# A two-layer graph attention kernel: masks built by ScalarE, a sum term in three bfloat16 parts, stacks loaded by fewer transfers, scores in column tiles

## The chip, the cores and the metric

The kernel runs on one core of a Trainium2 chip. The metric is the device time of one execution in microseconds (us); below it is the median of three runs. Lower is better.

## The reference, cut to what matters

Eight graphs (batches) of 1024 nodes with 128 features pass through two layers. Both use the same 0/1 adjacency matrix `adj`.

```python
# layer 0: 8 heads of 16 features
scores = einsum('bhqd,bhkd->bhqk', q, k) / sqrt(16)
w   = softmax(where(adj > 0, scores, -1e9))
x   = layernorm(x + (w @ v) @ Wo + bo)
# layer 1: one head
h   = x @ W.T
e   = leaky_relu(h @ a1 [:, :, None] + h @ a2 [:, None, :], 0.2)
x   = layernorm(x + softmax(where(adj > 0, e, -9e15)) @ h)
```

## The kernel before, in words

Everything stays on one core. A **unit** is the scores of one head and one block of 128 keys against all 1024 queries. There are 64 units in a batch, and unit `u` stands at **position** `u` of its batch. A unit has these steps:

- TensorE multiplies a 97-row stack of keys with a 97-row stack of queries: two matmuls of 512 columns (L415). The 97 rows are six blocks of 16 rows (q and k split into bfloat16 parts) and one row that subtracts a bound from the scores.
- ScalarE takes the exponential out of the PSUM slot into `weights` (L584).
- Non-neighbours are masked in one of two ways, chosen per unit by the string `MASKED_BY`. With "m" TensorE adds the mask to the scores with two more matmuls (L420). With "s" VectorE multiplies the weights by the mask afterwards (L755). "m" stands at 27 of the 64 positions.
- After each four units (a quad, four heads of one key block) TensorE adds their product with the values to the accumulator `acc` (L441). These are eight matmuls of 17 columns which stand in the four column tiles of the array, so that four run side by side.

Before a batch's units can run, its q and k are split into three bfloat16 parts each, written to a scratch in HBM (`send_parts`) and read back as the stacks `qst` and `kst` (`load_stack`), once for heads 0 to 3 and once for heads 4 to 7. The masks are made from the int32 adjacency rows (`raw`, two buffers), one for each key block (`make_mask`, L780, VectorE).

While the units of batch b run, the rest of batch b-1 (output projection, layer norm, layer 1) and of b-2 (the products `out0` to `out7` of layer 1, L474, and their final layer norm) is done between them, and q, k and v of batch b+1. What stands behind which position is written out by hand in one table for each engine (`PE_AT`, `ACT_AT`, `DVE_AT`, `POOL_AT`, `SP_AT`); an entry `("out0", -2)` at position 1 means: behind unit 1 of batch b, output product 0 of batch b-2. Each engine runs its list in order and waits on semaphores. Units and all jobs of TensorE that need PSUM share three slots in turn, so TensorE can be at most three uses ahead of the engines that empty them.

Each output product sums eight fp32 matmuls, and a ninth (L475) adds a constant row, the sum over all nodes times a tiny number, which keeps rows without neighbours defined: `pe.matmul(to, ones[:], hsum[:], ...)`, an fp32 product over 128 rows of which 127 are zero.

Of the kernel before, what the change touches and what calls it, by code (L numbers as in the profile page):

```python
# [35 lines left out]
}  # L36
PE_AT = {
# [4 lines left out]
}  # L42
ACT_AT = {
# [17 lines left out]
}  # L61

OFFSET_BITS = -70
EXPONENT = 40.0
FARTHEST = 60.0
# [7 lines left out]
def context_at(b, pos, batches):  # L73

    if pos % 4 != 3:
        return None
# [1592 lines left out]
```

## Time and profile before

| | |
|---|---|
| median of 3 runs | 927.75 us (924.52 to 927.9) |
| profiled execution, its own time | 921.75 us |
| its span, first to last instruction | 920.0 us |
| mean granted TensorE clock | 0.972 |
| busy: TensorE, VectorE, ScalarE, GpSimd | 844.0, 686.2, 635.3, 65.5 us |
| first exponential of the first unit | 37.75 us |
| first batch, second, third to seventh (each), eighth | 79.9, 93.0, 106.4, 98.6 us |
| from the last exponential of a unit to the end | 78.8 us |

The last three lines are start times of exponentials (L584), of position 0 in each batch. PE in a row is TensorE's matmuls, PEld its weight loads, DVE VectorE, ACT ScalarE, POOL GpSimd, SP the engine that issues the transfers. A matmul in fp32 shows as two records in the profile.

### The profile page before, as it was taken

What the parts mean: (1) busy time and instruction counts of PE and PEld (TensorE: products, weight loads), DVE (VectorE), ACT (ScalarE), POOL (GpSimd) and SP (SyncE); (2) the same over time, 40 slices, a digit from 0 to 9 for tenths busy, and PEclk for the clock granted to TensorE, in tenths of its full rate; (3) what the DMA queues carried; (4) which work ended last, traced back from release to release, by engine and by line L of the source; (5) the groups of instructions that cost most, each with busy time, mean ns of one, the idle gap of its engine ahead of it and who ended that gap; (6) DMA issues with size and microseconds to landing.
All of it is one profiled execution on the core that took longest, in us unless ns stands there. A gap on an engine that the chain in (4) does not pass through costs nothing.

```text
span 920.0 us, 14889 instructions
## 1 busy us (share of the span) xinstructions
PE 844.0 (92%) x5485; PEld 406.5 (44%) x5485; DVE 686.2 (75%) x1157; ACT 635.3 (69%) x702; POOL 65.5 (7%) x47
## 2 busy tenths in 40 slices
PE   5499999999999999999999999999999999998683
PEld 2132334327533474336543374334743366324573
DVE  5276797895878868896878868787687966796463
ACT  2378886995579846896579945898378965796050
POOL 3000010001010100101010010101010010101000
PEclk9599999999999999999999999999999999999877
DMA  4877258603556227544377136363275234401000
GB/s 158 158 135 154 38 163 161 111 7 109 110 120 105 81 92 94 138 58 126 82 149 100 39 102 118 115 94 90 83 136 110 44 105 96 54 2 35 1 24 26
DMA packets 50926, 85.56 MB, mean 93 GB/s; under 512 B 5969, under 2 KB 23122, under 8 KB 50834
## 3 DMA queue, kind: packets, MB, share of 16 engines
q1 hardware_dynamic: 50850, 84.57, 44.2%
q8 instruction: 45, 0.74, 0.4%
q14 instruction: 31, 0.25, 0.1%
HBM read 67.63 MB, written 16.91 MB: 92 GB/s over the span
## 4 chain that ended last, share of the span: by engine, by line
PE 69%; ACT 16%; issue 8%; DVE 5%; DMA 0%; POOL 0%; POOLq 0%; SPq 0%; ACTq 0%; DVEq 0%
PE acc L441 18%; PE slot L415 17%; PE slot L474 11%; ACT weights L584 11%; PE slot L420 8%; ACT atts L602 4%; PE slot L485 3%; PE slot L522 2%; PE slot L532 2%; DVE weights L755 1%; PE slot L475 1%; PE slot L458 1%; PE slot L512 1%; DVE atts L769 1%; PE slot L526 1%
## 5 line engine op out<-in xcount | busy, mean ns | idle before, releaser
L584 ACT ACTIVATE weights<-slot 128x1024 f32<-128x1024 f32 x512 | 496.1, 1048 | 169.4 <-PE slot L415 94.1
L755 DVE SCALAR_TENSOR_TENSOR weights<-mask,weights 128x1024 f32<-128x1024 bf16 x296 | 359.3, 1239 | 65.4 <-ACT weights L584 64.2
L415 PE MATMUL slot<-qst,kst 97*128 97x512 bf16 x1024 | 287.3, 383 | 26.9 <-issue 14.6
L441 PE MATMUL acc<-weights,vst 128*17 128x512 f32 x2048 | 244.6, 595 | 7.1 <-DVE weights L755 6.5
L415 PEld LDWEIGHTS slot<-qst,kst 97*128 97x128 bf16 x1024 | 84.7, 98 | 213.2 <-ACT weights L584 87.2
L420 PE MATMUL slot<-mask,same 128*128 128x512 bf16 x432 | 129.8, 381 | 0.0
L474 PEld LDWEIGHTS slot<-hst,atts 128*128 128x128 f32 x896 | 105.8, 191 | 19.4 <-issue 9.2
L474 PE MATMUL slot<-hst,atts 128*128 128x129 f32 x896 | 110.7, 276 | 3.0 <-ACT atts L602 3.0
L441 PEld LDWEIGHTS acc<-weights,vst 128*17 128x17 f32 x2048 | 47.9, 96 | 141.1 <-issue 127.5
L769 DVE SCALAR_TENSOR_TENSOR atts<-turn,hst,mask 128x1024 f32<-128x1024 f32 x64 | 83.5, 1310 | 6.8 <-ACT hst L652 6.8
L845 DVE RECIPROCAL rout<-slot 128x1 f32<-128x1 f32 x62 | 10.4, 167 | 91.0 <-PE slot L475 82.4
L602 ACT ACTIVATE atts<-atts,expbias 128x1024 f32<-128x1024 f32 x64 | 75.4, 1224 | 1.7 <-DVE atts L769 1.1
L420 PEld LDWEIGHTS slot<-mask,same 128*128 128x128 bf16 x432 | 42.4, 98 | 52.1 <-issue 1.1
L708 POOL TENSOR_TENSOR rstd<-vareps,exponent 128x4 f32<-128x4 f32 (+1 forms) x24 | 33.9, 1413 | 393.6 <-DVE vareps L825 393.6
L713 POOL TENSOR_TENSOR x_sb<-x_sb,bo_all 128x1024 f32<-128x1024 f32 x8 | 22.5, 2808 | 437.9 <-DMA x_sb<-in_x 437.9
L780 DVE TENSOR_SCALAR mask<-raw 128x1024 bf16<-128x1024 int32 x64 | 48.1, 753 | 6.4 <-DMA raw<-in_adjT 6.4
L618 ACT ACTIVATE atts<-slot 128x1024 bf16<-128x1024 f32 x16 | 16.4, 1023 | 23.6 <-PE slot L485 23.6
L830 DVE TENSOR_SCALAR x<-y,meanvar,rstd 128x128 f32<-128x128 f32 x64 | 17.1, 343 | 14.5 <-POOL rstd L708 14.5
L793 DVE TENSOR_TENSOR atts<-slot,atts 128x1024 f32<-128x1024 f32 x16 | 19.6, 1224 | 11.2 <-issue 11.0
L641 ACT ACTIVATE turn<-slot 128x1024 f32<-128x1024 f32 x8 | 8.2, 1023 | 26.0 <-PE slot L518 26.0
L846 DVE SCALAR_TENSOR_TENSOR x<-slot,rout,x 128x128 f32<-128x128 f32 x62 | 21.8, 351 | 2.2
L864 DVE TENSOR_REDUCE widest<-slot 64x1 f32<-64x1024 f32 x8 | 9.7, 1216 | 17.2 <-issue 10.0
(117 smaller groups left out, 580.3 us busy)
## 6 DMA issues: line engine op xcount, KB each, us to landing
raw<-in_adjT SPq DMA_DIRECT2D x64, 512.0 KB, 4.1
parts_scratch<-atts SPq DMA_DIRECT2D x48, 256.0 KB, 2.5
qst<-parts_scratch SPq DMA_DIRECT2D x96, 128.0 KB
kst<-parts_scratch SPq DMA_DIRECT2D x96, 128.0 KB
xT_sb<-in_xT SPq DMA_DIRECT2D x8, 512.0 KB, 4.6
x_sb<-in_x SPq DMA_DIRECT2D x8, 512.0 KB, 5.4
out<-x SPq DMA_DIRECT2D x16, 256.0 KB, 2.3
qst<-shift_scratch SPq DMA_DIRECT2D x16, 8.0 KB
```

What stands on the lines that cost most here:

```text
L415: mm = pe.matmul(ps[:, cols], kst[:, h, t * 128:(t + 1) * 128], qst[:, h, cols], start=True, stop=not by_pe)
L420: mm = pe.matmul(ps[:, cols], same[:], masks[b % 2][:, t, cols], start=False, stop=True)
L441: mm = pe.matmul(acc[VW * i:VW * i + HD + 1, cols], vst[b % 2][:, t, g * HG + i], weights[:, HG * buffer(b, n) + i, cols], start=(t == 0), ...
L474: pe.matmul(to, att_of(j, k), hst[:, j, 0:D + 1], start=(j == 0), stop=False)
L485: mm = pe.matmul(ps[:, cols], (wq if name == "q" else wk)[:], xT_sb[:, cols], **kw)
L584: act.activation(to, ps[:], ACT.Exp, scale=SCALE).then_inc(exp_done, 1)
L602: act.activation(atts[:, :, j, :], atts[:, :, j, :], ACT.Exp, bias=expbias[:, j:j + 1]).then_inc(atts_made, 1)
L708: pool.tensor_tensor(rstd[i][:, tt], vareps[i][:, tt], exponent[:, tt], ALU.pow).then_inc(rstd_made[k], 1)
L713: pool.tensor_tensor(x_sb[:], x_sb[:], bo_all[:].unsqueeze(1).to_broadcast([128, T, D]), ALU.add).then_inc(xb_made, 1)
L755: dve.scalar_tensor_tensor(out=to, in0=masks[b % 2][:, n % T], scalar=0.0, in1=at, op0=ALU.is_equal, op1=ALU.mult).then_inc(masked, 1)
L769: dve.scalar_tensor_tensor(out=atts[:, :, j, :], in0=fi_all[:].rearrange("p (q n) -> p q n", q=4), scalar=hst[:, j, D + 1:D + 2], in1=mask ...
L780: dve.tensor_scalar(masks[b % 2][:, t], raw[m][:], 0, -BIG, ALU.is_le, ALU.mult).then_inc(masks_made, 1)
```

## The change

Five things are changed together.

- **Masks.** ScalarE makes them, as relu(BIG/2 - BIG x adj) from `raw`, behind its own units (`("mask1", 0)` at position 2 and so on in `ACT_AT`); VectorE makes none. The sign of the mask is turned, so the identity `same` of the "m" units is now -1.
- **Sum term.** The constant row is split by GpSimd into three bfloat16 parts, in rows 0, 32 and 64 of `hparts` (five small instructions a batch), and is added by one bfloat16 matmul over 65 rows with `pick`. To have the row in all three places, the last product of `h1` is 65 columns wide instead of one.
- **Stacks.** q's parts are written to HBM six times, in the order of the stack's six blocks, so that one transfer of 96 rows loads a half of `qst`; `kst` comes in three transfers of 48, 32 and 16 rows. With the bound's row that makes 5 transfers a half instead of 13. q, k and the bound wait for their own semaphores.
- **Column tiles.** 35 of the 64 units are multiplied in four column tiles of 32 keys: eight matmuls of 32 columns instead of two of 128, and so for their masks. 48 groups of eight in a batch are of this kind (35 of scores, 13 of masks).
- **Tables.** "m" stands at 21 positions, "s" at 42, "d" at one (the exponential stays in the slot and VectorE reads it there). Contexts follow one unit later, and nearly every job has another position.

```diff
+MASKED_BY = ("ssss" "sssm" "ssss" "ssss" "ssmm" "msms" "ssmm" "mssm" ...
+    2: [("mask1", 0)], 4: [("acc1", -1)], 8: [("mask2", 0)], 12: [("mask3", 0)], 14: [("ctxT", -1)],
...
+CONTEXT_AFTER = 8
+TILED = ("...." "t..." "t..." ".t.." "tttt" "tttt" "tt.." ".ttt" ...
+K_RUNS = ((0, 3), (3, 2), (5, 1))
+Q_COPIES = ((0, 1, 2), (3, 4), (5,))
...
-    STACK_DMAS = 2 * BLOCKS + 1
+    STACK_DMAS = 5
+    SUMS = 2 * VW + 1
...
                 for i in range(3):
-                    sp.dma_start(scratch[s, i].rearrange("h d n -> (h d) n"), parts[s][i]).then_inc(parts_out, 16)
+                    for to in [q_scratch[:, r] for r in Q_COPIES[i]] if s == 0 else [k_scratch[:, i]]:
+                        sp.dma_start(to, parts[s][i]).then_inc(parts_out[s], 16)
...
-                for r in range(BLOCKS):
-                    rows = slice(r * HD, (r + 1) * HD)
-                    sp.dma_start(qst[rows, heads], scratch[0, QPART[r], heads].rearrange("h d n -> d h n")).then_inc(stack_in[g], 16)
-                    sp.dma_start(kst[rows, heads], scratch[1, KPART[r], heads].rearrange("h d n -> d h n")).then_inc(stack_in[g], 16)
+                if what == "q":
+                    sp.wait_ge(parts_out[0], (b + 1) * 96)
+                    sp.dma_start(qst[0:KROWS, heads], q_scratch[heads].rearrange("h i d n -> (i d) h n")).then_inc(stack_in[g], 16)
+                elif what == "k":
+                    sp.wait_ge(parts_out[1], (b + 1) * 48)
+                    for r, n in K_RUNS:
+                        sp.dma_start(kst[r * HD:(r + n) * HD, heads],
+                                     k_scratch[heads, 0:n].rearrange("h i d n -> (i d) h n")).then_inc(stack_in[g], 16)
...
+                if TILED[u] == "t":
                     for c in range(2):
+                        cols = slice(c * HALF, (c + 1) * HALF)
+                        for i in range(4):
+                            rows = slice(VW * i, VW * (i + 1))
+                            keys = slice(t * 128 + VW * i, t * 128 + VW * (i + 1))
+                            mm = pe.matmul(ps[rows, cols], kst[:, h, keys], qst[:, h, cols], start=True, stop=not by_pe)
...
-                    pe.matmul(to, ones[:], hsum[:], start=False, stop=True).then_inc(full[name], 1)
+                    pe.matmul(to, pick[:], hparts[:], start=False, stop=True).then_inc(full[name], 1)
...
+            def make_mask(b, t):
+                if b > 1:
+                    act.wait_ge(atts_summed, (b - 1) * T)
+                m = t % RAW
+                act.wait_ge(raw_in[m], (b * (T // RAW) + t // RAW + 1) * 16)
+                act.activation(masks[b % 2][:, t], raw[m][:], ACT.Relu, bias=cutoff[:], scale=-BIG).then_inc(masks_made, 1)
```

TensorE in a batch in the middle, from the third context on (position 15 before, 16 now). In the rows before, L415 are scores, L420 masks, L441 the context, L518 and L522 transposes and output projection, L485 k.

```order
L441 MATMUL acc<-weights,vst 17x512 x8
L518 MATMUL slot<-ident,turn 128x128 x8
L415 MATMUL slot<-qst,kst 128x512 x2
L420 MATMUL slot<-mask,same 128x512 x2
L415 MATMUL slot<-qst,kst 128x512 x2
L522 MATMUL slot<-wo,turn 128x128 x8
```

In the rows now, L441 are tiled scores, L446 tiled masks, L474 the context, L557 the output projection, L509 and L510 an output product with its sum term.

```order
L474 MATMUL acc<-weights,vst 17x512 x8
L441 MATMUL slot<-qst,kst 32x512 x8
L557 MATMUL slot<-wo,turn 128x128 x8
L509 MATMUL slot<-hst,atts 128x129 x8
L510 MATMUL slot<-hparts,pick 128x129
L441 MATMUL slot<-qst,kst 32x512 x8
L446 MATMUL slot<-mask,same 32x512 x8
```

The projection now stands ahead of an output product, and a unit has eight matmuls of 32 columns where it had two of 128.

ScalarE from position 57 of one batch over its end into the next, before (L584 exponentials of units, L602 of layer 1, L630 and L637 the values, L596 the accumulator):

```order
L602 ACTIVATE atts<-atts,expbias 128x4x256 x2
L584 ACTIVATE weights<-slot 128x1024 x2
L630 ACTIVATE vst<-slot 128x32x16
L637 ACTIVATE vbias<-slot,denbias 128x2
L584 ACTIVATE weights<-slot 128x1024 x2
L602 ACTIVATE atts<-atts,expbias 128x4x256 x2
L584 ACTIVATE weights<-slot 128x1024 x6
L596 ACTIVATE turn<-acc,vbias 128x1024
```

The same now, from position 61 (L619 exponentials of units, L645 of layer 1, L676 and L683 the values, L627 a mask):

```order
L619 ACTIVATE weights<-slot 128x1024 x2
L676 ACTIVATE vst<-slot 128x32x16
L645 ACTIVATE atts<-atts,expbias 128x4x256 x2
L619 ACTIVATE weights<-slot 128x1024
L676 ACTIVATE vst<-slot 128x32x16
L683 ACTIVATE vbias<-slot,denbias 128x2
L627 ACTIVATE mask<-raw,cutoff 128x1024
L619 ACTIVATE weights<-slot 128x1024 x3
L627 ACTIVATE mask<-raw,cutoff 128x1024
```

Both halves of the values, the last two exponentials of layer 1 and the next batch's first mask now stand close together at positions 62 and 63.

SP at the start of the program, before; ten more transfers like the last two follow, and then the bound's row:

```order
L384 DMA bo_all<-in_bo 128x128
L327 DMA parts_scratch<-atts 128x1024 x6
L334 DMA shift_scratch<-negshift 8x1024
L345 DMA qst<-parts_scratch 16x4x1024
L346 DMA kst<-parts_scratch 16x4x1024
```

The same now:

```order
L342 DMA q_scratch<-atts 8x16x1024 x6
L342 DMA k_scratch<-atts 8x16x1024 x3
L349 DMA shift_scratch<-negshift 8x1024
L359 DMA qst<-q_scratch 96x4x1024
L367 DMA qst<-shift_scratch 1x4096
L363 DMA kst<-k_scratch 48x4x1024
L363 DMA kst<-k_scratch 32x4x1024
L363 DMA kst<-k_scratch 16x4x1024
```

k's parts stand ahead of the bound (`shift`), which waits behind them in SP's list, and VectorE's second step for k (`k1`) now stands behind its maximum for the bound (`cc`).

## Rows read from the trace of the kernel before

**Rows 1.** Windows: length, then busy us of PE, PEld, DVE, ACT, POOL; clock; DMA.

```profile
37.74:117.61 79.87, 77.91 (x455) 25.88 (x454) 57.06 (x58) 65.73 (x71) 0.00 (x0) 0.97 0.59 120
117.61:210.62 93.01, 90.07 (x559) 35.44 (x558) 77.48 (x100) 78.35 (x87) 4.77 (x2) 1.00 0.53 111
...
423.41:529.80 106.39, 103.80 (x685) 50.03 (x684) 84.84 (x143) 79.06 (x87) 6.92 (x4) 1.00 0.49 101
742.58:841.17 98.59, 94.21 (x628) 43.71 (x630) 77.17 (x132) 73.75 (x80) 10.22 (x5) 1.00 0.29 58
841.17:920.00 78.83, 50.26 (x386) 44.45 (x374) 36.57 (x131) 16.03 (x18) 5.73 (x5) 0.81 0.05 15
```

**Rows 2.** Windows: the fifth batch, positions 0 to 39 and 40 to 63.

```profile
423.40:496.90 73.50, 73.02 (x489) 38.44 (x488) 57.16 (x113) 47.51 (x52) 6.92 (x4) 1.00 0.52 113
496.90:529.80 32.90, 30.79 (x198) 11.59 (x197) 27.69 (x30) 31.56 (x35) 0.00 (x0) 1.00 0.42 74
```

**Rows 3.** Timeline inside positions 40 to 63: start, us, engine and line.

```profile
399.52 3.82 ACT L584 ACTIVATE weights<-slot 128x1024 f32<-128x1024 f32 x4
...
401.56 0.60 PE L415 MATMUL slot<-qst,kst 97*128 97x512 bf16 x2 [0.31 <-ACT weights L584]
...
402.01 0.60 PE L420 MATMUL slot<-mask,same 128*128 128x512 bf16 x2
402.53 0.13 PEld L441 LDWEIGHTS acc<-weights,vst 128*17 128x17 f32 x8 [0.42 <-ACT weights L584]
402.53 1.91 PE L441 MATMUL acc<-weights,vst 128*17 128x512 f32 x16
...
403.13 1.24 ACT L602 ACTIVATE atts<-atts,expbias 128x1024 f32<-128x1024 f32 x1
...
404.17 2.94 ACT L584 ACTIVATE weights<-slot 128x1024 f32<-128x1024 f32 x3
...
404.38 1.04 PE L415 MATMUL slot<-qst,kst 97*128 97x512 bf16 x4
```

**Rows 4.** Timeline of an output product, its sum term, and the next product.

```profile
429.82 1.95 PE L474 MATMUL slot<-hst,atts 128*128 128x129 f32 x16
431.60 0.39 PE L475 MATMUL slot<-hsum,ones 128*128 128x129 f32 x2
431.82 1.95 PE L474 MATMUL slot<-hst,atts 128*128 128x129 f32 x16
```

**Rows 5.** Timeline of the bound's product, four matmuls in two column tiles.

```profile
478.46 0.60 PE L492 MATMUL slot<-atts,headsum 128*32 128x512 bf16 x4
478.99 0.61 PE L415 MATMUL slot<-qst,kst 97*128 97x512 bf16 x2
```

**Rows 6.** Groups by line: busy us, mean ns of one, idle before them.

```profile
L755 DVE SCALAR_TENSOR_TENSOR weights<-mask,weights 128x1024 f32<-128x1024 bf16 x296 | 359.3, 1239 | 65.4 <-ACT weights L584 64.2
...
L780 DVE TENSOR_SCALAR mask<-raw 128x1024 bf16<-128x1024 int32 x64 | 48.1, 753 | 6.4 <-DMA raw<-in_adjT 6.4
```

**Rows 7.** Timeline of SP's queue: first and last of the 13 stack transfers.

```profile
21.76 0.33 SPq L345 DMA_DIRECT2D qst<-parts_scratch  x1
...
27.29 0.28 SPq L347 DMA_DIRECT2D qst<-shift_scratch  x1
```

**Rows 8.** Windows at the start: parts written, then stacks loaded (last: DMA share, GB/s).

```profile
13.00:21.00 8.00, 5.75 (x35) 4.07 (x35) 7.90 (x13) 1.90 (x7) 0.00 (x0) 1.00 0.53 197
21.70:34.50 12.80, 0.36 (x2) 0.27 (x2) 0.22 (x2) 0.26 (x1) 0.56 (x1) 0.53 0.99 122
```

**Rows 9.** Chain of waits at the start: start, us, what.

```profile
36.70 2.72 PE slot L415 x6
```

**Rows 10.** Timeline at the start: VectorE's maximum for the bound.

```profile
17.63 1.21 DVE L864 TENSOR_REDUCE widest<-slot 64x1 f32<-64x1024 f32 x1
```

**Rows 11.** Chain of waits behind the last unit.

```profile
863.04 1.03 ACT turn L641
...
902.41 0.46 PE slot L460 x4
```

More of the change, by code:

```diff
@@ L73, in context_at @@
 def context_at(b, pos, batches):
-    if pos % 4 != 3:
-        return None
-    me, n = (b - 1, 15) if pos == 3 else (b, (pos - 7) // 4)
-    return (me, n) if 0 <= me < batches else None
+    me, n = (b, pos - CONTEXT_AFTER) if pos >= CONTEXT_AFTER else (b - 1, pos + UNITS - CONTEXT_AFTER)
+    return (me, n // 4) if n % 4 == 0 and 0 <= me < batches else None
 def ring_plan(batches):
@@ L153, in build_fast @@
         half = sb("half", [128, 1], F32)
+        cutoff = sb("cutoff", [128, 1], F32)
         usq = sb("usq", [D, 2], F32)
@@ L412, in unit @@
                 by_pe = MASKED_BY[u] == "m"
-                for c in range(2):
-                    cols = slice(c * HALF, (c + 1) * HALF)
-                    mm = pe.matmul(ps[:, cols], kst[:, h, t * 128:(t + 1) * 128], qst[:, h, cols], start=True, stop=not by_pe)
                 if by_pe:
                     pe.wait_ge(masks_made, b * T + t + 1)
+                if TILED[u] == "t":
                     for c in range(2):
+                        cols = slice(c * HALF, (c + 1) * HALF)
[3 more added lines that the diff above has]
+                            mm = pe.matmul(ps[rows, cols], kst[:, h, keys], qst[:, h, cols], start=True, stop=not by_pe)
+                    for c in range(2 if by_pe else 0):
+                        cols = slice(c * HALF, (c + 1) * HALF)
+                        for i in range(4):
+                            rows = slice(VW * i, VW * (i + 1))
+                            mm = pe.matmul(ps[rows, cols], same[:, rows], masks[b % 2][:, t, cols], start=False, stop=True)
+                else:
+                    for c in range(2):
+                        cols = slice(c * HALF, (c + 1) * HALF)
+                        mm = pe.matmul(ps[:, cols], kst[:, h, t * 128:(t + 1) * 128], qst[:, h, cols], start=True, stop=not by_pe)
+                    for c in range(2 if by_pe else 0):
                         cols = slice(c * HALF, (c + 1) * HALF)
@@ L458, in last_outs @@
                         pe.matmul(attention_of(me, k), att_of(j, k), hst[:, j, 0:D + 1], start=(j == 0), stop=False)
+                pe.wait_ge(hsum_split, me + 1)
                 for k in range(T):
-                    pe.matmul(attention_of(me, k), ones[:], hsum[:], start=False, stop=True).then_inc(full[f"out{k}"], 1)
+                    pe.matmul(attention_of(me, k), pick[:], hparts[:], start=False, stop=True).then_inc(full[f"out{k}"], 1)
             def job(name, me):
@@ L606, in job @@
                     read_acc(me, int(name[3]))
+                    return
+                if name[:4] == "mask":
+                    make_mask(me, int(name[4]))
                     return
@@ L682, in _, with link @@
         def _(pool):
+            chain = {"n": 6}
+            def link(ins):
+                chain["n"] += 1
+                ins.then_inc(pool_step, 1)
+                pool.wait_ge(pool_step, chain["n"])
             pool.memset(ones[:], 1.0)
-            pool.memset(same[:], 1.0)
+            pool.memset(same[:], -1.0)
             pool.memset(headsum[:], NORM_WEIGHT).then_inc(pool_step, 1)
@@ L699, in _ @@
             pool.memset(half[:], 0.5)
+            pool.memset(cutoff[:], BIG / 2.0)
             pool.memset(exponent[:], -0.5).then_inc(pool_step, 1)
             pool.wait_ge(pool_step, 5)
+            pool.memset(pick[:], 0.0).then_inc(pool_step, 1)
+            pool.wait_ge(pool_step, 6)
+            for i in range(3):
+                link(pool.memset(pick[VW * i:VW * i + 1], 1.0))
             pool.memset(kst[KROWS:SROWS], 1.0).then_inc(consts_made, 1)
@@ L708, in inverse_root, with split_sum @@
                 pool.tensor_tensor(rstd[i][:, tt], vareps[i][:, tt], exponent[:, tt], ALU.pow).then_inc(rstd_made[k], 1)
+            def split_sum(b):
+                pool.wait_ge(taken["h1"], b + 1)
+                for t in range(T):
+                    pool.wait_ge(full[f"out{t}"], b)
+                second, third = slice(VW, 2 * VW), slice(2 * VW, SUMS)
+                link(pool.tensor_copy(hparts[:, 1:D + 1], hsum[:]))
+                link(pool.tensor_tensor(hrest, hsum[:], hparts[:, 1:D + 1], ALU.subtract))
+                link(pool.tensor_copy(hparts[second, 1:D + 1], hrest[second]))
+                link(pool.tensor_copy(hparts[third, 1:D + 1], hrest[third]))
+                pool.tensor_tensor(hparts[third, 1:D + 1], hrest[third], hparts[third, 1:D + 1],
+                                   ALU.subtract).then_inc(hsum_split, 1)
+                pool.wait_ge(hsum_split, b + 1)
             def residual(b):
```

56 lines of the change are left out of this document (35 added, 21 removed), and 40 rows, old and new, of tables (ACT_AT, DVE_AT, PE_AT, SP_AT).

## The prediction, made before the changed kernel had run

> **What bounds the kernel now.** I read the windows first, batch by batch. From the third batch on a batch takes 106.39 us, and TensorE's matmuls are busy for 103.80 of them, VectorE for 84.84, ScalarE for 79.06 [rows 1]. A busy TensorE need not be one that works, so I looked at the two halves of a batch. In positions 0 to 39, where the output products and projections stand, TensorE is busy for 73.02 of 73.50 us and ScalarE for 47.51. In positions 40 to 63 ScalarE is busy for 31.56 of 32.90 us [rows 2]. The timeline of that half shows it: exponentials start 0.90 us apart (four from 399.52 to 403.13), and scores wait 0.31 us for ScalarE to free a slot [rows 3]. So TensorE sets the pace for 70% of a batch and ScalarE for the rest; VectorE sets it nowhere.
>
> The first batch has none of the later jobs and takes 79.87 us, the second 93.01, the eighth 98.59, and behind the last exponential there are 78.83 us [rows 1] in which one batch goes alone through its chain. At the start TensorE's first scores come at 36.70 us [rows 9]: until then they wait for the stack.
>
> **Prices, from the rows.** Two 512-column matmuls take 0.45 us (401.56 to 402.01); I use 0.44. A context takes 1.85 us, and the step from 128 columns into the column tiles adds 0.08 us (402.01 to 402.53 less 0.44) [rows 3]. The sum term takes 0.22 us in its two fp32 records (431.60 to 431.82) [rows 4]. An exponential holds ScalarE 0.90 us, and one that reads and writes SBUF and takes its bias from a tile 1.04 us (403.13 to 404.17) [rows 3]. VectorE's masking takes 1.24 us, its mask 0.75 [rows 6].
>
> **Masks by TensorE.** There are 27 "m" units before and 21 now: six times 0.44 = 2.6 us of TensorE a batch. By position it is 20 to 12 in positions 0 to 39 (-3.5 us) and 7 to 9 in the rest (+0.9, where ScalarE sets the pace).
>
> **Sum term.** A 129-column bfloat16 product in one pass is not in the trace; 512 columns take 0.22 us, so 129 take 0.055 at that rate, and at most the 0.22 of now. I take 0.06: 0.16 x 8 = 1.3 us a batch. GpSimd's five steps are hidden: it idles most of a batch (6.92 us busy) [rows 1], and the sum is wanted half a batch later.
>
> **Column tiles.** 48 groups a batch become eight matmuls. The bound's product shows four bfloat16 matmuls in two column tiles in 0.53 us, the step out of the tiles included, so two ran side by side [rows 5]; the fp32 contexts run four. I price a group at its old 0.44 us plus 0.01 for tiles that start after one another: +0.5 us a batch. Steps between the two shapes are 34 a batch both before and now, as I count the written order, so nothing is saved or lost there. The price from above is under the rivals.
>
> **Masks by ScalarE.** This kind of instruction (int32 in, bfloat16 out) is not in the trace; the nearest rows are 1.04 us (SBUF to SBUF, bias tile) and 0.90. I take 1.04: +8.3 us a batch on ScalarE, which idles for 27 us of a batch. VectorE loses 8 x 0.75 = 6.0 us and gains six maskings, 7.4: no change that matters, it has over 20 us to spare. Behind a mask on ScalarE its exponentials queue, and for them TensorE's slots. The adjacency rows come at least two masks ahead, and four positions or more lie between the mask that frees a buffer and the one that reads it, so I see no new wait on transfers.
>
> **A batch in the middle.** Positions 0 to 39 on TensorE: -3.5 (masks) -1.3 (sums) +0.4 (tiles) +1.9 (product `out1`, which moves from position 63 to 14) = -2.5 us. Seven of the eight masks stand there beside ScalarE's idle time. Positions 40 to 63 on ScalarE: one more mask, +1.0. But its last five items (both halves of the values, two layer-1 exponentials, the mask) now stand at positions 62 and 63, beside a context and `out0` (1.85 and about 1.85 us) that TensorE can do meanwhile: stepping through the slots, TensorE loses about 0.6 us there instead of the 3 that ScalarE is over, so -1.5 for this half. Against it: the bound's product moves from position 27 to 30 on TensorE, and ScalarE's copy of it to the same position, so ScalarE stands for VectorE's maximum (1.2 us [rows 10]) where it had a unit between: +1.0. Sum -3.0 us, bounds -5 (no such loss) and 0 (nothing hidden at positions 62 and 63). Five such batches: **-15**.
>
> **The other batches.** The second has no output products; ScalarE, 78.35 busy of 93.01 [rows 1], becomes 86.7, and I take half of TensorE's 3.5: -1.8. The first: -0.5, since ScalarE, now 74 of 79.87, takes over most of its length. The eighth has no mask for a next batch: -2.5.
>
> **The tail.** Eight output products of the seventh batch stood ahead of the last projection; now seven do, one of them beside ScalarE's copy (1.03 us [rows 11]) that TensorE waited for, and each is 0.16 shorter: -2.0 -1.2 -1.1. The eighth now stands behind the projection, and VectorE waits for it before its statistics: +1.2. One context more is behind the last exponential: +1.0. The eight sum terms at the end (two of them 0.46 us [rows 11]): -1.3. The last two normalisations no longer lie beside GpSimd: +0.9. Sum **-2.5**.
>
> **The start.** The 13 transfers are issued from 21.76 to 27.57 us [rows 7] and move 1.6 MB at 122 GB/s with the transfer engines busy for 0.99 of the time, while 128-row transfers, also of 2 KB pieces, got 197 GB/s at a share of 0.53 [rows 8]: the same engines could give over twice as much, so the 16-row shape is what is slow. The Trainium skill has the reason (SBUF — State Buffer, "Door 1: The DMA port swizzle"): a transfer's rate goes by how many of 16 ports its partitions reach, 4 for 16 rows and all 16 for rows 0 to 95. No run shows the 96-row shape.
>
> At the rates between, 1.6 MB take 4.3 (at 372, the 197 at full share) to 13 us. What begins later: `k1` behind the maximum (17.63 + 1.21, [rows 10]) ends at about 21, three transfers of k's parts and then the bound go out until 23, and k's stack, which stands behind the bound's row, at 25 to 27 us. Landing at 28.5 at best gives -8, at the old rate 0. q's parts are now six writes whose outer dimension is 8, and the bound queues behind all of it. I take **-6**. On that shape the skill (DMA: Bandwidth & Descriptors, on how many engines a transfer uses) says that it runs on 8 of 16 engines; no row here shows it.
>
> **Sum.** -6 -0.5 -1.8 -15 -2.5 -2.5 = -28.3 against the execution's own 921.75 us: 893.5, or 0.969. On the median of 927.75, which lies 6 above that execution, it is **899 us**.
>
> **Rivals.** *ScalarE takes the pace.* For it: 87 us of 103, in three places in lumps. If nothing is hidden at positions 62 and 63 a middle batch gains 0, the first two lose 2 and 1, the last gains 1: with start and tail -6.5, so 921. Against it: 20 us of idle time remain, and seven masks stand beside TensorE's longest jobs. Chance 0.15.
>
> *The stacks load no faster* (the rate is the scratch's, or q's six writes hold up the bound): no -6, so 905. Against it is the share of 0.99 beside 0.53. Chance 0.09.
>
> *TensorE can't issue the tiles fast enough*, which ends on the other side. A tiled group is 16 instructions (8 loads, 8 matmuls) in 0.44 us, 27 ns each. The trace shows eight loads within 0.13 us after a wait, but over a stretch no more than a context's 32 in 1.85 us, 57 ns each [rows 3], and there the array was the limit. At 57 ns a group costs 0.91: +0.47 x 48 x 8 = +180 us. It decides at 0.074 us a group (28.3/384), that is at 32 ns an instruction; at 40 ns it is +0.2 x 384 = +77, some of it beside ScalarE's half: about 965. Nothing shows such a limit, and nothing shows its absence. Chance 0.14, of it 0.03 for a small cost (0.50 us a group, +23: 922). The skill (TensorE: Matmul & The Clock Gate, "Wait — 56ns, not 53.3ns?") names such a cost, about 62 ns a matmul where the sequencer decodes them; eight would be the 0.50.
>
> *More is hidden* (the bound's move costs nothing and TensorE alone sets the pace): -5 a middle batch, 885 or less. Chance 0.07.
>
> **How the numbers follow.** 0.55 remain for my forecast, with a range of its own of 885 to 912. A measurement tells 0.5% from no change, so faster is under 923: 0.55 + 0.07 + 0.09 + 0.10 of the first rival = 0.81; the same: its other 0.05 and the small issue cost, 0.08; slower: 0.11. The range of 8 in 10, 880 to 925, leaves out the issue limit and the deepest gain.
>
> **What would show it.** First scores at 28 to 33 us (36.70 now); stacks at 250 GB/s or more. Tiled groups 0.44 us after one another when nothing waits; more than 0.5 is the issue limit. The sum term 0.06 us. A middle batch of 102 to 104 us, with positions 0 to 39 at 71 and the rest at 32 to 33; ScalarE busy for some 87. I am wrong if ScalarE has no gaps in positions 0 to 39, or if a batch stands at 106.

## The result, and the profile after

The changed kernel takes 897.1 us (median of 4, 893.61 to 898.16) against 926.13 us of the kernel before on the same chip (4 runs): a ratio of 0.968, with an interval of 0.964 to 0.972. The prediction was 899. Its profiled execution takes 896.19 us, 25.6 less than the 921.75 of before (the medians are 29.0 apart); the stretches in this section are those of the two executions. A line of its page has engine, busy us (share of the span) and instructions.

```profile
PE 814.8 (91%) x7597; PEld 398.1 (45%) x7629; DVE 698.0 (78%) x1141; ACT 701.9 (78%) x766; POOL 118.2 (13%) x92
```

The windows of the same stretches as in [rows 1] (first, second, fifth, eighth batch, tail; length, busy us of PE, PEld, DVE, ACT, POOL, clock, DMA) say where the time went:

```profile
42.48:122.60 80.12, 76.33 (x726) 25.14 (x728) 62.31 (x57) 73.13 (x80) 2.75 (x1) 0.95 0.51 129
122.60:215.15 92.55, 87.18 (x830) 34.65 (x827) 79.55 (x96) 86.70 (x97) 10.46 (x7) 1.00 0.46 118
419.33:521.46 102.13, 99.61 (x950) 48.88 (x953) 86.25 (x140) 87.53 (x96) 14.39 (x10) 1.00 0.44 112
725.73:819.76 94.03, 90.94 (x907) 43.93 (x909) 75.50 (x131) 81.35 (x88) 10.18 (x10) 1.00 0.25 66
819.76:894.20 74.44, 44.77 (x358) 40.33 (x358) 37.59 (x132) 16.00 (x18) 15.14 (x11) 0.84 0.06 16
```

| stretch | predicted | measured |
|---|---|---|
| start, to the first exponential | -6 | +4.7 (37.75 to 42.48) |
| first batch | -0.5 | +0.3 |
| second batch | -1.8 | -0.5 |
| five middle batches | 5 x -3.0 | 5 x -4.3 |
| eighth batch | -2.5 | -4.6 |
| tail | -2.5 | -4.4 |
| sum | -28.3 | -25.8 |

The total came close because two errors cancel: the start lost 10.7 us against its term, and middle batches, eighth batch and tail gained 10.3 more than theirs.

In the middle TensorE is still the one that is full, 99.61 of 102.13 us, 4.2 fewer than before. The two halves of the fifth batch, as in [rows 2]:

```profile
419.33:488.70 69.37, 68.47 (x604) 36.80 (x609) 54.94 (x107) 55.01 (x60) 4.47 (x4) 1.00 0.48 133
488.70:521.46 32.76, 31.14 (x350) 12.07 (x344) 31.32 (x34) 32.52 (x38) 9.92 (x6) 1.00 0.35 68
```

In positions 0 to 39 ScalarE, now with the masks, is busy for 55 of 69 us, so they lie in its idle time. In positions 40 to 63 ScalarE has 0.24 us left and VectorE 1.4; VectorE had 5.2 before.

The prices per piece are seen in the timeline of TensorE (start, us, engine and line). Two tiled groups (L441, x16) start at 402.41 and their masks at 403.29, so 0.44 us a group, 27 ns for each of its 16 instructions. The sum term (L510) is followed by the next matmul after 0.06 us; in [rows 4] it was 0.22.

```profile
402.41 1.05 PE L441 MATMUL slot<-qst,kst 97*32 97x512 bf16 x16
403.29 0.61 PE L446 MATMUL slot<-mask,same 128*32 128x512 bf16 x8
...
420.12 0.22 PE L510 MATMUL slot<-hparts,pick 65*128 65x129 bf16 x1
420.18 0.38 PE L450 MATMUL slot<-qst,kst 97*128 97x512 bf16 x1
```

The start is where the prediction failed. In the timeline of VectorE and of SP's queue, the maximum for the bound (L941) comes at 20.55 where [rows 10] have 17.63, after 4.47 us of waiting for the bound's product; k's last subtraction (L876) stands behind it; k's parts leave at 24.01; the first stack transfer goes out at 27.41 where [rows 7] have 21.76, and k's three transfers at 32.98, behind a bound's row that SP had to wait for.

```profile
20.55 1.22 DVE L941 TENSOR_REDUCE widest<-slot 64x1 f32<-64x1024 f32 x1 [4.47 <-PE slot L527]
...
22.76 1.23 DVE L876 TENSOR_TENSOR atts<-atts 128x1024 bf16<-128x1024 f32 x1
...
14.10 6.17 SPq L342 DMA_DIRECT2D q_scratch<-atts  x6
24.01 1.93 SPq L342 DMA_DIRECT2D k_scratch<-atts  x3
...
27.41 2.13 SPq L359 DMA_DIRECT2D qst<-q_scratch  x1
32.71 0.23 SPq L367 DMA_DIRECT2D qst<-shift_scratch  x1
32.98 1.26 SPq L363 DMA_DIRECT2D kst<-k_scratch  x3
```

The chain of waits agrees ([rows 9] had 36.70): it shows no work between 26.00 and the first scores.

```profile
26.00 15.43 issue
41.43 1.02 PE slot L450 x2
```

### The profile page after: what moved, and what is told of

The parts are those of the page before. It is cut to its first block, busy times and chain, and to the rows that moved or that the text cites. A ratio compares the mean times of both kernels' runs of the same rounds, so it can differ in the third digit from the quotient of the medians.

```text
span 894.2 us, 19419 instructions
## 1 busy us (share of the span) xinstructions
PE 814.8 (91%) x7597; PEld 398.1 (45%) x7629; DVE 698.0 (78%) x1141; ACT 701.9 (78%) x766; POOL 118.2 (13%) x92
## 4 chain that ended last, share of the span: by engine, by line
PE 67%; ACT 16%; issue 10%; DVE 5%; DMA 0%; POOL 0%; ACTq 0%; POOLq 0%; SPq 0%; DVEq 0%
PE acc L474 17%; ACT weights L619 12%; PE slot L509 12%; PE slot L441 9%; PE slot L450 9%; PE slot L520 3%; PE slot L446 3%; PE slot L453 2%; ACT atts L645 2%; PE slot L557 2%; DVE x L907 2%; PE slot L575 2%; PE slot L567 2%; PE slot L547 2%; PE slot L491 1%
## 5 line engine op out<-in xcount | busy, mean ns | idle before, releaser
L619 ACT ACTIVATE weights<-slot 128x1024 f32<-128x1024 f32 x504 | 491.7, 1041 | 77.3 <-PE slot L450 39.4
L831 DVE SCALAR_TENSOR_TENSOR weights<-mask,weights 128x1024 f32<-128x1024 bf16 x336 | 403.4, 1235 | 53.7 <-ACT weights L619 43.4
L474 PE MATMUL acc<-weights,vst 128*17 128x512 f32 x2048 | 243.3, 593 | 0.0
L441 PE MATMUL slot<-qst,kst 97*32 97x512 bf16 x2240 | 160.5, 383 | 5.8 <-ACT weights L619 5.2
L450 PE MATMUL slot<-qst,kst 97*128 97x512 bf16 x464 | 133.6, 388 | 27.2 <-issue 15.4
L509 PEld LDWEIGHTS slot<-hst,atts 128*128 128x128 f32 x896 | 106.8, 191 | 17.4 <-ACT weights L619 9.6
L509 PE MATMUL slot<-hst,atts 128*128 128x129 f32 x896 | 110.5, 276 | 3.2 <-issue 1.7
L474 PEld LDWEIGHTS acc<-weights,vst 128*17 128x17 f32 x2048 | 52.3, 97 | 119.5 <-issue 96.8
L441 PEld LDWEIGHTS slot<-qst,kst 97*32 97x32 bf16 x2240 | 49.6, 95 | 115.8 <-ACT weights L619 49.3
L450 PEld LDWEIGHTS slot<-qst,kst 97*128 97x128 bf16 x464 | 35.6, 100 | 112.9 <-ACT weights L619 58.3
L645 ACT ACTIVATE atts<-atts,expbias 128x1024 f32<-128x1024 f32 x64 | 75.4, 1203 | 2.6 <-DVE atts L846 2.0
L627 ACT ACTIVATE mask<-raw,cutoff 128x1024 bf16<-128x1024 int32 x64 | 74.6, 1165 | 0.0
L787 POOL TENSOR_TENSOR x_sb<-x_sb,bo_all 128x1024 f32<-128x1024 f32 x8 | 35.7, 4464 | 222.4 <-DMA x_sb<-in_x 222.4
L446 PE MATMUL slot<-mask,same 128*32 128x512 bf16 x832 | 63.2, 379 | 0.0
L922 DVE RECIPROCAL rout<-slot 128x1 f32<-128x1 f32 x62 | 10.3, 166 | 58.8 <-PE slot L510 53.8
L453 PE MATMUL slot<-mask,same 128*128 128x512 bf16 x96 | 31.4, 381 | 2.0 <-issue 0.2
L446 PEld LDWEIGHTS slot<-mask,same 128*32 128x32 bf16 x832 | 22.5, 97 | 22.6
```

Of the source, the lines that this page charges most:

```text
L441: mm = pe.matmul(ps[rows, cols], kst[:, h, keys], qst[:, h, cols], start=True, stop=not by_pe)
L446: mm = pe.matmul(ps[rows, cols], same[:, rows], masks[b % 2][:, t, cols], start=False, stop=True)
L450: mm = pe.matmul(ps[:, cols], kst[:, h, t * 128:(t + 1) * 128], qst[:, h, cols], start=True, stop=not by_pe)
L453: mm = pe.matmul(ps[:, cols], same[:], masks[b % 2][:, t, cols], start=False, stop=True)
L474: mm = pe.matmul(acc[VW * i:VW * i + HD + 1, cols], vst[b % 2][:, t, g * HG + i], weights[:, HG * buffer(b, n) + i, cols], start=(t == 0), ...
L509: pe.matmul(to, att_of(j, k), hst[:, j, 0:D + 1], start=(j == 0), stop=False)
```

## The experiments

e1 to e4 ran on one chip, e5, e6, e10 and e11 on a second and the others on a third, each beside runs of the kernel before, whose median there stands in the table. I started from this theory: TensorE's fewer maskings and cheaper sum terms make the gain, the column tiles are worth nothing, the masks lie in idle time, and the new stack transfers save no time at the start. The rivals give the gain to the tiles, or to ScalarE's masks.

| kernel | us | before | ratio (interval) |
|---|---|---|---|
| changed kernel | 897.1 | 926.1 | 0.968 (0.964 to 0.972) |
| e1, no tiles | 893.7 | 924.1 | 0.967 (0.964 to 0.969) |
| e2, 20 steps a batch | 896.3 | 924.1 | 0.968 (0.964 to 0.973) |
| e3, 13 stack transfers | 890.7 | 924.1 | 0.963 (0.959 to 0.966) |
| e4, masks on VectorE | 922.9 | 924.1 | 0.999 (0.997 to 1.001) |
| e5, fp32 sum term | 907.4 | 924.7 | 0.980 (0.978 to 0.983) |
| e6, k's parts ahead of the maximum | 899.8 | 924.7 | 0.972 (0.969 to 0.974) |
| e10, 27 units on TensorE | 962.0 | 924.7 | 1.041 (1.038 to 1.043) |
| e11, the same, masks on VectorE | 1001.8 | 924.7 | 1.081 (1.077 to 1.085) |
| e14, e11 with masks made early | 940.8 | 923.5 | 1.019 (1.016 to 1.022) |
| e15, e14 with 21 units | 900.6 | 923.5 | 0.974 (0.970 to 0.979) |
| e7, e1 + e3 + start mended | 885.9 | 923.5 | 0.959 (0.956 to 0.962) |
| e7b, e7 with the new stacks | 893.9 | 923.5 | 0.966 (0.963 to 0.969) |

### Column tiles: e1 and e2

e1, and then e2 (strings put on one line here and below):

```diff
-TILED = ("...." "t..." "t..." ".t.." "tttt" "tttt" "tt.." ".ttt" ...
+TILED = ("................" "................" "................" "................")
```

```diff
-TILED = ("...." "t..." "t..." ".t.." "tttt" "tttt" "tt.." ".ttt" ...
+TILED = ("t...ttt.tt..ttt." "tt..tttttttttttt" "t...tttttttttttt" "ttttttttttttttt.")
```

> All scores by two 512-column matmuls (no unit in column tiles), the rest as in the changed kernel. My theory: the tiles are worth nothing by themselves, since a group takes the same 0.41 to 0.44 us and there are 34 steps between the two shapes a batch either way: 897 within 4 us, a middle batch at 102 us. Rival, the tiles give the gain of the change (TensorE is fed sooner, or more columns run at once): a middle batch goes back by 2 us or more, the time to 912 or above.

> Tiled units chosen so that a batch has 20 steps between untiled and tiled work instead of 34 (51 tiled units instead of 33). A step is about 0.1 us in the trace. Theory: 14 steps fewer are -1.4 us a batch at most where TensorE sets the pace, and nothing in positions 40 to 63, where ScalarE does: 2 to 11 us less, 886 to 895. Rival, steps are hidden in the queue of the array or tiles cost something of their own: the same 897 or, at 0.03 us for each of 18 more tiled groups, +4.

e1 is not slower than the changed kernel (893.7 against 897.1, the intervals of the ratios overlap), and its fifth batch takes 101.87 us against 102.13: the tiles are worth nothing, and cost at most 0.3 us a batch. The prediction's +0.4 was right in sign. e2 has 51 tiled units against 35 (not the 33 of the expectation). Its batches take 101.84 us, the same as e1's, and the whole 896.3: the 2 to 11 us that I expected of fewer steps between the two shapes aren't there, as the rival had it. If 35 tiled units cost the 0.26 us, 51 cost 0.4, so 14 steps fewer can have saved 0.4 us a batch at most (an estimate).

### The sum term: e5

```diff
-                    pe.matmul(to, pick[:], hparts[:], start=False, stop=True).then_inc(full[name], 1)
+                    pe.matmul(to, ones[:], hsum[:], start=False, stop=True).then_inc(full[name], 1)
...
-                if name == "hsum":
-                    split_sum(me)
```

> The sum term goes back to one fp32 product of 128 rows, without GpSimd's split. Theory by the prediction's term: 0.16 us for each of 64 products, +1.3 us a middle batch and about as much behind the last exponential: +9 to +13, so 906 to 910. Rival, most of it is hidden or the record understates what the term holds: +3 or less, or +16 and more.

907.4 us, within the expectation. The window of its fifth batch gives +1.5 us on 102.13, with TensorE 1.7 us busier; the prediction's term was 1.3.

```profile
419.71:523.35 103.64, 101.35 (x962) 50.21 (x961) 85.78 (x140) 87.77 (x96) 9.07 (x5) 1.00 0.41 111
```

### The masks: e4, e10, e11, e14, e15

e4 gives the masks back to VectorE at the positions where ScalarE made them, two of them one position earlier. From `ACT_AT` into `DVE_AT`:

```diff
-    2: [("mask1", 0)], 4: [("acc1", -1)], 8: [("mask2", 0)], 12: [("mask3", 0)], 14: [("ctxT", -1)],
...
+    2: [('mask1', 0)],
+    5: [('out4', -2)],
+    7: [('mask2', 0), ('ctx1', -1)],
...
+    11: [('mask3', 0)],
```

> VectorE makes the eight masks (0.75 us each) at the positions where ScalarE made them (two of them one position earlier), ScalarE makes none. Theory: the gain of the change is TensorE's six maskings fewer, and both engines have room for the masks: VectorE gets to 93 us of 102, ScalarE to 79, the time stays within 6 us of 897, rather above it. Rival 1, masks on ScalarE are what made the gain (VectorE's queue was late): a middle batch goes back by 2 us or more, 912 or above. Rival 2, the masks on ScalarE cost time in positions 40 to 63 and at the batch's start: 890 or less.

922.9: the whole gain was gone, which my theory did not allow and rival 1 did. But the waits of TensorE in its fifth batch (line waited for: us, times, longest) show another cause than a full VectorE. Scores that TensorE masks itself wait 2.3 us for the mask, nearly all of the 2.5 us by which that batch is longer (104.64).

```profile
PE slot L490 <- DVE mask L897: 1.8, 1, 1.8
...
PE slot L481 <- DVE mask L897: 0.5, 1, 0.5
```

A unit masked by TensorE needs its mask before the exponential, a unit masked by VectorE after it, and the changed tables make each mask 0 to 5 positions ahead of its first unit. In the tables before it was 5 to 14 (not the 8 to 20 of e14's expectation). e10 asked what six more maskings on TensorE cost, and e11 joined it with e4:

```diff
-MASKED_BY = ("ssss" "sssm" "ssss" "ssss" "ssmm" "msms" "ssmm" "mssm" "sssm" "smsm" "sssm" "ssmm" "mssm" "ssdm" "mssm" "sssm")
+MASKED_BY = ("ssms" "msms" "smss" "ssmm" "msmm" "mmsm" "mmmm" "ssss" "ssms" "smmm" "ssss" "smss" "smsm" "smss" "ssms" "msms")
```

> TensorE masks 27 units of a batch as in the kernel before (the same positions), ScalarE makes the masks as in the changed kernel. Theory by the prediction's term: +2.6 us of TensorE a batch, 8 units more of it in positions 0 to 39 (+3.5 where TensorE sets the pace) and 2 fewer in the rest (0 to -0.9): +2.6 to +3.5 a middle batch, 916 to 923. Rival, ScalarE or VectorE share the pace so that TensorE's share counts little: +1 a batch or less, 897 to 906.

> 27 units masked by TensorE and the masks made by VectorE, both as in the kernel before; order, sums, tiles and stacks of the changed kernel. With 21 such units masks on VectorE cost 25 us. Theory: what cost there was VectorE's queue (90.9 us busy of 104.6, scores waiting for its masks), and 27 units relieve it of 7.4 us a batch but give TensorE 2.6: a middle batch 104 to 105.5, the whole 912 to 922, no better than with 21. So a mask on ScalarE is worth its place only because it buys VectorE the six maskings. Rival, VectorE's masks cost by their place in its order whatever the number of maskings: 930 or above.

962 and 1002 us, e10 far above both expectations and e11 in its rival's: the 27 positions of before stand where the mask is not made yet. In e10's first batch, which has no later jobs in it, TensorE's waits are

```profile
PE slot L441 <- ACT mask L627: 3.7, 2, 2.3
PE slot L450 <- ACT mask L627: 2.4, 2, 1.4
```

against 0.2 us for masks in the changed kernel's first batch; and that batch takes 87.8 us instead of 80.1. So neither run prices a masking. e14 and e15 make the masks early, on VectorE at the positions of before, with 27 and with 21 units on TensorE; the last adjacency rows are loaded earlier to match. Of `DVE_AT`:

```diff
+    0: [('mask2', 0)],
...
+    5: [('out4', -2), ('mask3', 0)],
+    7: [('ctx1', -1), ('mask4', 0)],
...
+    13: [('mask6', 0)],
```

> The whole mask part undone: 27 units masked by TensorE and the masks made by VectorE, all at the positions of the kernel before (VectorE's masks 8 to 20 positions ahead of their first unit, adjacency rows loaded as early); the rest is the changed kernel. In the two runs that gave 962 and 1002 TensorE waited for masks that are made right beside their first unit, because the old positions of TensorE's units stood beside the new positions of the masks. Theory: with masks early that wait is gone and only the price of six maskings on TensorE is left, +2.6 to +3.5 a middle batch: 912 to 922. Rival, the order of the changed kernel is what needs the new positions: 935 or more.

> Masks made by VectorE at the early positions of the kernel before, with the changed kernel's 21 units on TensorE. Theory 1: the 25 us that masks on VectorE cost at the late positions were their lateness; made early they cost nothing but 6 us of an engine with room: 895 to 905. Theory 2: they were VectorE's load (90.9 us of 104.6, in stretches without a gap): 912 to 925 as before, and then ScalarE's masks are what lets TensorE give up six.

e15 settles the place of the masks: made early on VectorE the whole takes 900.6 us, theory 1. Its middle batches take 102.15 us, as with ScalarE. The profiled executions differ in the second batch (96.5 against 92.6 us), so ScalarE's masks may be worth a few us in all; the two intervals, 0.970 to 0.979 and 0.964 to 0.972, overlap. Of e4's 25 us, 22 were lateness.

e14 differs from e15 in the string alone and takes 108.4 us for its fifth batch. The halves of the fifth batch in e14:

```profile
434.78:508.20 73.42, 72.39 (x654) 39.40 (x664) 51.53 (x107) 48.47 (x54) 6.89 (x4) 1.00 0.41 119
508.20:543.18 34.98, 30.15 (x320) 10.41 (x314) 32.09 (x35) 31.65 (x37) 4.61 (x6) 1.00 0.37 78
```

and in e15:

```profile
420.59:491.00 70.41, 69.52 (x613) 37.89 (x618) 58.92 (x115) 48.25 (x54) 6.10 (x4) 1.00 0.44 124
491.00:522.74 31.74, 30.11 (x342) 10.99 (x335) 31.59 (x35) 31.50 (x37) 9.01 (x6) 1.00 0.38 86
```

Positions 0 to 39 differ by 3.0 us, with TensorE 2.9 us busier: the prediction's 3.5 for eight maskings, nearly. Positions 40 to 63 differ by 3.2 us, and there TensorE is equally busy. There contexts wait 2.6 us for VectorE's maskings in e14, whose string has two more of them in this half. But VectorE is busy for only 32.09 of 34.98 us. Ahead of the maskings it waits 3.2 us for k's writes, and in e14 the chain of waits runs through that:

```profile
502.30 6.96 DMA k_scratch<-atts
...
509.36 1.31 DVE atts L895
```

e15 has the same wait (3.3 us), and its chain does not run through it. So the two units and this wait may both have a part in the 3.2 us; no run tells them apart. The prediction gave the two units +0.9. My 912 to 922 fell to this, and the rival (935 or more) held: the string belongs to the order. With the old string the new order is the slower one (108.4 us a batch against 106.39 before), although its sum terms save 1.5.

### The start and the stacks: e3, e6, e7, e7b

e3 goes back to one scratch, six writes and 13 loads a half, in the changed kernel's order:

```diff
-                    for to in [q_scratch[:, r] for r in Q_COPIES[i]] if s == 0 else [k_scratch[:, i]]:
-                        sp.dma_start(to, parts[s][i]).then_inc(parts_out[s], 16)
+                    sp.dma_start(scratch[s, i].rearrange("h d n -> (h d) n"), parts[s][i]).then_inc(parts_out[s], 16)
...
-                    sp.dma_start(qst[0:KROWS, heads], q_scratch[heads].rearrange("h i d n -> (i d) h n")).then_inc(stack_in[g], 16)
+                    for r in range(BLOCKS):
+                        sp.dma_start(qst[r * HD:(r + 1) * HD, heads],
+                                     scratch[0, QPART[r], heads].rearrange("h d n -> d h n")).then_inc(stack_in[g], 16)
```

e6 moves one entry of VectorE's table:

```diff
-    18: [("stats3", -2), ("q0", 1)], 20: [("q1", 1)], 21: [("k0", 1), ("norm1", -1)], 25: [("aggr3", -2)],
-    26: [("stats2", -2)], 27: [("cc", 1)], 31: [("k1", 1)], 32: [("xsum", 1)], 34: [("aggr2", -2), ("h0", -1)],
+    18: [("stats3", -2), ("q0", 1)], 20: [("q1", 1)], 21: [("k0", 1), ("norm1", -1)], 24: [("k1", 1)], 25: [("aggr3", -2)],
+    26: [("stats2", -2)], 27: [("cc", 1)], 32: [("xsum", 1)], 34: [("aggr2", -2), ("h0", -1)],
```

e7b moves it ahead of the first batch only, loads the bound's row behind k's stack and has no tiles; e7 is the same with e3's transfers:

```diff
+DVE_START = {**DVE_AT, 24: [("k1", 1)], 31: []}
...
-                    for name, me in jobs_at(DVE_AT, b, pos, B):
+                    for name, me in jobs_at(DVE_AT if b >= 0 else DVE_START, b, pos, B):
...
-    40: [("stackk0", 1), ("store0", -2)], 42: [("x", 0), ("raw2", 1)], 51: [("raw3", 1)], 52: [("raw4", 1)],
+    40: [("stackk0", 1), ("stackr0", 1), ("store0", -2)], 42: [("x", 0), ("raw2", 1)], 51: [("raw3", 1)], 52: [("raw4", 1)],
```

> The stacks go back to one scratch and 13 transfers of 16 rows for each half of the heads, in the changed kernel's order. Theory: at the start the faster load of k's stack (24 us earlier issue to first scores) is paid back by q's six writes on half of the transfer engines and by a bound that queues behind k's writes, so the start moves by less than 4 us either way and the batches not at all: 893 to 902. Rival 1, the new shape saves what I predicted (about 6 us) and something else delays the start: 903 to 910. Rival 2, the six writes are what delays the start: 888 to 892.

> VectorE finishes k's parts (position 24) ahead of the bound's maximum (27); the changed kernel has them behind it (31), where at the start VectorE idles 4.5 us for the bound's product and the parts leave at 24 us. Theory: parts of k leave behind q's at about 20 us, the first scores come 2 to 5 us sooner than at 41.4 us, the batches stay within 0.3 us each: 892 to 896. Rival 1, q's writes and the bound hold the stack up anyway: first scores at 40 us or more, 897. Rival 2, the order of middle batches suffers (the maximum and the bound come later): 900 or more.

> No unit in column tiles, 13 stack transfers of 16 rows, k's parts made ahead of the bound's maximum in the first batch alone, the shift row loaded behind k's stack. Each part alone was worth 0 to 6 us. Theory: first scores at 37 to 38.5 us, second batch 91.2, middle batches 101.9: 884 to 889. Rival, the parts overlap (the start is bound by the load alone): 890 or more.

> The same without the 13 transfers: the changed kernel's nine writes and five loads for the stacks. Theory: its writes (2.4 MB at half of the transfer engines) hold up the load by 3 to 5 us, and its load is 2 to 3 us shorter: first scores 0 to 3 us later than with 13 transfers, the second batch 1.4 later where VectorE waits for k's writes: 886 to 892, 2 to 4 above the other. Rival, without the shift row ahead of k's stack the new shape is the faster: 2 us or more below the other.

e3 took 890.7, below the 893 to 902 of the theory and inside rival 2: the old transfers look the better ones (the two intervals still touch; e7 and e7b below are apart). e6 took 899.8, rival 2: its first exponential came at 39.79 (42.48 in the changed kernel, 40.7 in e1, whose start is the same), but every middle batch grew by 0.9 us. Why is seen at ScalarE's copy of the bound. In the changed kernel it waits 0.45 us:

```profile
475.31 1.10 ACT L670 ACTIVATE negshift<-slot,negkmax 8x1024 bf16<-8x1024 f32 x1 [0.45 <-issue]
```

and in e6 2.18 us, because k's cast and subtraction (0.68 and 1.23 us) now stand ahead of VectorE's maximum:

```profile
474.75 1.10 ACT L670 ACTIVATE negshift<-slot,negkmax 8x1024 bf16<-8x1024 f32 x1 [2.18 <-issue]
```

TensorE then waits 0.9 us for that copy, which is what the batch grew by:

```profile
PE slot L567 <- ACT negshift L670: 0.9, 1, 0.9
```

So e7 and e7b move that entry ahead of the first batch only. They differ in the stacks alone, 885.9 and 893.9: with the new stacks the kernel is 8 us slower, where I expected 2 to 4. SP's queue at the start of e7, then the chain's first scores:

```profile
14.44 5.15 SPq L341 DMA_DIRECT2D parts_scratch<-atts  x6
...
22.45 2.67 SPq L359 DMA_DIRECT2D qst<-parts_scratch  x6
...
35.66 1.03 PE slot L451 x2
```

and of e7b:

```profile
14.03 6.57 SPq L343 DMA_DIRECT2D q_scratch<-atts  x6
20.65 3.93 SPq L343 DMA_DIRECT2D k_scratch<-atts  x3
...
25.80 1.33 SPq L360 DMA_DIRECT2D qst<-q_scratch  x1
29.87 1.26 SPq L364 DMA_DIRECT2D kst<-k_scratch  x3
...
38.95 1.03 PE slot L451 x2
```

From the first load to the first scores both take 13.2 us (35.66 - 22.45, and 38.95 - 25.80). The new stacks move faster, but k's can't go out before k's writes have landed, and SP waits 2.7 us of the 13.2 for that (until 29.87). The windows (last two columns: share of the transfer engines, GB/s) show the rate, first e7 and then e7b, with q's 96 rows and the first of k's:

```profile
26.00:29.00 3.00, 0.00 (x0) 0.00 (x0) 0.00 (x0) 0.00 (x0) 0.00 (x0) 0.50 1.05 137
```

```profile
29.00:32.00 3.00, 0.00 (x0) 0.00 (x0) 0.00 (x0) 0.00 (x0) 0.00 (x0) 0.50 1.04 259
```

From 32 to 35 us, with the rest of k's (48, 32 and 16 rows), e7b moves 160 GB/s. So the load gains about what it waits, and the 3.3 us at the start come from ahead of it: nine writes end their issue at 24.58 where six ended at 19.59.

The second batch is 1.7 us longer too (92.8 against 91.08): VectorE waits there 3.8 us in the changed kernel, and 4.1 in e7b, before it writes `atts`, in whose space the parts lie until they are sent. With 13 transfers the wait is not there, nor in e6, where k's parts are ready earlier, and the second batch of e6 takes 91.15 us too. The lines of the changed kernel's waits, in the second batch and in the fifth:

```profile
DVE atts L846 <- issue: 3.8, 1, 3.8
```

```profile
DVE atts L846 <- DMA k_scratch<-atts: 3.4, 1, 3.4
```

In the middle batches the same wait costs nothing: they take 102.15 us in e3, without it, and 102.13 in the changed kernel.

The two profiled executions differ by 9.6 us. What is left beside the 3.3 and 1.7 is 1.8 in the first batch and 2.5 in the tail, and both go with the granted clock: from 44 to 47 us e7 has 0.84 and e7b 0.50, and over the last eight products 1.00 and 0.90. So 5.0 of the 9.6 us are traced to the stacks; the tail's part is no work of theirs. e7 is the best kernel of the study, 1% below the changed one.

## Why the prediction was right, and where it was wrong

**The start (-6, measured +4.7): the failed step.** Three parts of it fell.

- "three transfers of k's parts and then the bound go out until 23" left out how long nine writes take. SP has issued them at 25.9, and where k's parts are ready sooner, still only at 24.6 (e7b).
- `k1` was to end "at about 21", behind a maximum taken at 17.63. The maximum now waits openly for the bound's product, behind which VectorE's own work on k had lain. It came at 20.55, and `k1` ended at 24. That was in part the clock (last section): in e2, whose start is the same, it came at 17.78, and the first load still went out only at 26.04, the first exponential at 40.73, 3.0 us later than before.
- The rate was right for q's 96 rows (the forecast 250 GB/s or more; 259), not for k's three transfers (160), and k's load had to wait for k's writes. So the new shape won nothing in e7b beside e7.

The rival "the stacks load no faster" (0.09) was right in the time and in its remark on q's six writes, not in the rate. By the first exponential 13 transfers alone win 0.8 us (39.89 against e1's 40.73, although e3's maximum came at 20.33 and e1's at 19.32), the order alone 0.7 (e7b's 40.00), both 4.0 (e7's 36.71).

**A middle batch (-3.0, measured -4.27): right in mechanism, one term mis-sized.** TensorE's busy time fell by 4.2 us, which six maskings (2.6 at their price) and the sums (1.5 by e5) make up. The term that failed is the +1.0 for the bound's product: ScalarE stood for 0.45 us only, since the new order puts VectorE's maximum ahead of k's second step; e6 turns that around and pays 0.9. Without that term the sum was -4.0. Its split by halves was off: -4.1 fell in positions 0 to 39 and -0.1 in the rest. A part of that is `out0`, which I booked in the second half without taking it out of the first: TensorE begins it at 418.23 us, 1.1 us ahead of the fifth batch's first exponential. No run moved it alone. (The rival of *more is hidden*, -5 a middle batch, is 889 by the sum and not 885.)

**Prices.** Tiled groups 0.44 us, sum term 0.06 us, ScalarE 87.5 busy against "some 87": as priced. A mask holds ScalarE for 1.04 us, from its start at 45.20 to the next exponential at 46.24, as estimated. TensorE took 27 ns an instruction, so the rival of the issue limit (0.14) is out. The Trainium skill (TensorE: Matmul & The Clock Gate, "Wait — 56ns, not 53.3ns?") has about 62 ns a matmul where the sequencer decodes them; that would be 0.50 a group, and these rows show 0.44. ScalarE did not take the pace in positions 0 to 39 (55 of 69 us).

**"No change that matters" for VectorE** was right: over the batch VectorE is 1.4 us busier, as priced, and the place of the masks does not matter to a middle batch (e15). In positions 40 to 63 VectorE was 27.69 us busy [rows 2] and is 31.32 now, but most of that is work that its wait for k's writes pushed there. In e3, without the wait, it is busy for 28.21 us, and the half is as long:

```profile
485.57:518.25 32.68, 31.10 (x351) 12.03 (x344) 28.21 (x31) 32.44 (x37) 8.82 (x6) 1.00 0.29 53
```

**Second batch (-1.8, measured -0.5).** With 13 transfers it is 91.2 (e3), -1.8: the term was right, and the new wait for the writes took 1.4 of it. The prediction had looked for new waits at the adjacency rows alone. Why that wait costs time in this batch and not in the middle ones, no run shows.

**Eighth batch (-2.5, measured -4.6).** Mis-sized like the middle ones. e5 gives the sums 1.5 (95.6 us against 94.0), and the string is worth 4.0 in the new order (94.8 in e15, 98.8 in e14); the rest no run takes apart.

**Tail (-2.5, measured -4.4).** The windows up to the last eight products, over them, and behind, of before:

```profile
841.17:886.38 45.21, 32.44 (x242) 26.82 (x231) 19.73 (x76) 8.09 (x12) 3.69 (x3) 0.85 0.02 7
886.38:902.90 16.52, 16.52 (x134) 16.52 (x135) 8.20 (x12) 7.94 (x7) 0.00 (x0) 0.91 0.06 17
902.90:920.00 17.10, 1.30 (x12) 1.10 (x10) 8.65 (x45) 0.00 (x0) 2.04 (x2) 0.61 0.11 34
```

and of after:

```profile
819.76:861.30 41.54, 29.81 (x223) 25.55 (x223) 19.39 (x73) 8.10 (x12) 9.44 (x6) 0.88 0.01 2
861.30:876.10 14.80, 14.80 (x136) 14.78 (x136) 9.72 (x16) 7.91 (x7) 3.69 (x4) 1.00 0.12 37
876.10:894.20 18.10, 0.17 (x3) 0.00 (x0) 8.48 (x44) 0.00 (x0) 2.01 (x2) 0.63 0.12 32
```

The end behind the products is 1.0 longer (+0.9 was priced; no run moves the normalisations alone). The products took 1.7 less where 1.3 were given to their sums, but the clock has a part in that: granted 1.00 over them in this execution and 0.91 before. The stretch ahead of them won 3.7 where the terms sum to -2.1; why, no run shows.

## What to carry to other kernels

Where a hand-written order lets one engine make what another needs, an edit of who uses it can't be priced by instructions alone: six maskings more on TensorE, 2.6 us of its time, cost 6.2 us a batch with the masks made early (e14 beside e15) and 7.5 with the masks late (e10 beside the changed kernel). A load in fewer, wider pieces has to be priced together with the writes that it asks for, on the engines that these can use, and with the wait between the writes and the load. And where an operation is moved ahead of another in an engine's list, ask when its input is ready, not when it ran before.

## What the runs showed of the hardware

**Writes whose outer dimension is 8.** While the parts are written as 8 x 16 x 1024 in the changed kernel, the transfer engines stay at a share of 0.52, window after window (last two columns: share, GB/s):

```profile
17.00:20.00 3.00, 3.00 (x13) 1.77 (x11) 0.00 (x0) 0.00 (x0) 0.00 (x0) 0.50 0.52 176
20.00:23.00 3.00, 3.00 (x16) 2.57 (x13) 2.35 (x5) 0.97 (x1) 0.00 (x0) 0.50 0.52 193
```

The same bytes written as 128 x 1024, in e3, pass that:

```profile
14.00:17.00 3.00, 2.71 (x4) 1.19 (x5) 1.88 (x4) 0.00 (x0) 0.00 (x0) 0.50 0.71 262
```

The Trainium skill (DMA: Bandwidth & Descriptors, "Why a DMA increments its semaphore by 16 and not by 1", on how many engines a transfer uses) says that such a transfer runs on 8 of 16 engines; the flat 0.52 agrees.

**The clock between executions.** The same instructions are granted either level of the clock (0.50 is 1.2 GHz, 1.00 is 2.4) at the same place. At the start of the changed kernel TensorE ran at 0.50 from 14.1 to 24 us after an idle 3 us, and the bound's product ended at 20.5. Before, after an idle 3.5 us, it ran at 1.00 and the product ended at 17.4. Two runs have the changed kernel's start: in e1 the product ended at 19.3, and in e2, which ran at 1.00 there, at 17.7, so that the maximum came nearly as early as in [rows 10]:

```profile
17.78 1.22 DVE L941 TENSOR_REDUCE widest<-slot 64x1 f32<-64x1024 f32 x1 [1.63 <-PE slot L527]
```

In both the first exponential comes at 40.73 us. So 3.0 of the +4.7 us at the start stay at full clock, and the other 1.7 go with the clock of that one execution. In the tail the last eight products begin at half speed in some kernels' executions and not in others, and the tail takes from 73.6 us (e1) to 77.8 (e6) with the same instructions there. I can tie neither to a difference of the programs.
